# Expert weights from a PSUM bank, and the steps of dt by transfers, in a four-batch decoder kernel

## What is computed

```python
x = _layernorm(x + _L0_attn_ref(x, ...))            # state-space scan, 1024 channels x 16 states
x = _layernorm(x + _L0_xattn_ref(x, fside, ctx))    # two int8-quantised linears
x = _layernorm(x + _L0_ffn_ref(x, ...))             # gated feed-forward, 2048 hidden
x = _layernorm(x + _L1_attn_ref(x, ...))            # recurrence of another kind, 32 heads
x = _layernorm(x + _L1_xattn_ref(ctx, x, ...))      # state-space scan, 512 channels x 16 states
x = _layernorm(x + _L1_ffn_ref(x, ...))             # 8 experts of 352, top 2, and a shared one of 1408
```

```python
dt = softplus(ts @ dt_proj_w + dt_proj_b);  A = -exp(A_log)
h  = exp(dt_t * A) * h + (dt_t * x_t) * B_t          # for each position t
...
C   = top-2 routing weights of each token, one column for each of 8 experts
out = sum_e C[:, e] * swiglu_e(x) + sigmoid(x @ Wsg) * swiglu_shared(x)
```

## Time and profile before

| | |
|---|---|
| median of 3 runs | 4341.19 us (4337.18 to 4343.31) |
| profiled execution, its own time | 4338.52 us |
| its span | 4336.7 us |
| PE busy | 3493.1 us |
| DVE busy | 3340.8 us |
| ACT busy | 1365.5 us |
| POOL busy | 1277.1 us |
| granted clock, mean | 0.893 |

### The profile page before, as it was taken

How to read it: one execution, slowest core, us unless ns; L and a number is a source line. 1 busy time by engine, 2 the same in 40 slices (tenths; PEclk the granted TensorE clock), 3 DMA queues, 4 the chain that set the end, 5 groups by cost and what they waited for, 6 DMA issues and landing times. The chain is left out here.

```text
span 4336.7 us, 40016 instructions
## 1 busy us (share of the span) xinstructions
PE 3493.1 (81%) x14699; PEld 1469.8 (34%) x14967; DVE 3340.8 (77%) x2930; ACT 1365.5 (31%) x2006; POOL 1277.1 (29%) x452
## 2 busy tenths in 40 slices
PE   5777759887899859887899858877899968974898
PEld 2222233333333333333333333323333333322444
DVE  5998469777899668778899758868799858867444
ACT  4666333124322233224322233213422143121101
POOL 1544204331344203342244303343244312332000
PEclk9888879898899979989799978989799978976899
DMA  4888302121122302222122201122122301210232
GB/s 154 303 319 315 148 22 81 68 83 54 66 73 73 119 16 73 68 82 69 58 74 73 110 32 66 67 82 78 44 73 73 124 32 59 73 58 15 73 102 75
DMA packets 72917, 393.38 MB, mean 91 GB/s; under 512 B 8080, under 2 KB 8208, under 8 KB 70288
## 3 DMA queue, kind: packets, MB, share of 16 engines
q1 hardware_dynamic: 69264, 384.44, 25.5%
q10 hardware_dynamic: 3456, 6.29, 0.4%
HBM read 320.45 MB, written 70.25 MB: 90 GB/s over the span
## 5 line engine op out<-in xcount | busy, mean ns | idle before, releaser
L261 PE MATMUL ps<-r,ring 128*128 128x512 bf16 (+2 forms) x1989 | 781.4, 393 | 45.1 <-POOL r L244 22.5
L1025 POOL TENSOR_TENSOR hh<-hh,bc 128x2048 f32<-128x2048 f32 x72 | 337.2, 4683 | 1070.9 <-DVE hh L950 1070.9
L258 PE MATMUL ps<-r,ring 128*128 128x512 bf16 (+1 forms) x1349 | 540.4, 401 | 107.6 <-DVE xc L990 38.4
L258 PE MATMUL ps<-xr,ring 128*128 128x512 bf16 x1536 | 607.4, 395 | 11.5 <-DMA ring<-wsplit 8.8
L262 PE MATMUL ps<-xr,ring 128*128 128x512 bf16 x1533 | 604.2, 394 | 2.6
L262 PE MATMUL ps<-r,ring 128*128 128x512 bf16 (+2 forms) x1355 | 542.5, 401 | 2.0
L910 ACT ACTIVATE da<-ps,params_sb 128x511 f32<-128x511 f32 x768 | 463.2, 691 | 72.1 <-PE ps L816 33.6
L1025 POOL TENSOR_TENSOR bc<-bc 128x2048 f32<-128x2048 f32 x64 | 299.5, 4679 | 375.6 <-DVE bc L950 375.6
L1025 POOL TENSOR_TENSOR r<-r,bc 128x2048 f32<-128x2048 f32 x56 | 263.2, 4701 | 327.3 <-DVE r L950 327.3
L950 DVE TENSOR_TENSOR_SCAN hh<-da,hh 128x2048 f32<-128x2048 f32 x72 | 330.5, 4590 | 1.5
L917 ACT ACTIVATE row<-ps 128x512 f32<-128x512 f32 x100 | 59.7, 597 | 764.7 <-PE ps L262 764.7
(11 more groups left out here) (241 smaller groups left out, 6367.4 us busy)
## 6 DMA issues: line engine op xcount, KB each, us to landing
ring<-wsplit SPq DMA_DIRECT2D x304, 768.0 KB, 4.3
r<-wstream SPq DMA_DIRECT2D x76, 768.0 KB, 7.4
wsplit<-ring SPq DMA_DIRECT2D x58, 768.0 KB, 4.5
wsplit<-r SPq DMA_DIRECT2D x18, 768.0 KB, 5.7
r<-xT SPq DMA_DIRECT2D x7, 1024.0 KB, 4.8
r<-gates_dram SPq DMA_DIRECT2D x3, 2048.0 KB, 8.4
bc<-guwT SPq DMA_DIRECT2D x4, 1024.0 KB, 7.1
out<-xr SPq DMA_DIRECT2D x4, 1024.0 KB, 3.9
```

The costliest lines, as they stand in the source:

```text
L258: mm = pe.matmul(out, w_hi, x_hi, start=start, stop=False)
L261: pe.matmul(out, w_hi, x_lo, start=False, stop=False)
L1025: pool.tensor_tensor(quartet(s), quartet(s), k.out_rows, ALU.mult).then_inc(read, 1)
```

## The change

- `k.gates` (nine copies in SBUF) goes. `k.weight_rows` keeps the turned rows in SBUF, and in the expert stage PE spreads a tile's weights into a PSUM bank, from which `times_weight` reads. With scan steps this is bank 0 alone: `weight_spreads` lists the rows of the bank that change from one tile to the next (17 spreads over the 33 tiles), and `times_weight` is one instruction for each tile. A spread waits until the tile before has been multiplied. In the last batch three banks take turns, one spread for each of 9 experts, and `times_weight` keeps its pieces.
- Bank 0 was `dt_bank`. In the expert stage with scan steps dt now comes by transfers: ACT issues four of 32 rows for each step (`fetch`), into the first quarter of `da`, after scan(s-2); three exponentials read that quarter, and a fourth overwrites it once they are done. `a0` is rescaled by 1/16 once, before the batches, as the spread's factor is gone.
- In `hidden_and_scan`, `spread_dtx(1)` comes before `up(0)` rather than after it, in every stage.
- In `close_batch`: the nine spreads and nine copies go; dt products 4 and 5 with their `magnitude` and `positive` move ahead of the logits; the first half of the logits waits for half of the norm; the four low halves of the expert stage's input are made here, after line 1868, and no longer at the start of that stage; `logarithm(1)` comes before the copy of the rows.

```diff
+def weight_spreads(tile):
+    if tile == ROUTED:
+        return [(0, P, NEXP)]
+    if tile > ROUTED:
+        return []
+    held = lambda row: (tile * P - P + row) // FEXP if tile else None
+    return [(a, b, e) for a, b, e in expert_pieces(tile) if held(a) != e]
...
+            def spread_weights(jt):
+                q = 32 * ((jt + 3) % 4)
+                for a, b, e in new_weights(jt):
+                    if blocks and jt >= 1:
+                        pe.wait_ge(weighted, jt)
+                    elif not blocks and e >= 3:
+                        pe.wait_ge(weighted, expert_tiles(e - 3)[-1] + 1)
+                    pe.matmul(weight_bank(e)[a:b, :], k.ident[q:q + 32, q + e:q + e + 1].broadcast_to([32, b - a]),
+                              k.weight_rows[q:q + 32, :], start=True, stop=True).then_inc(spread_mm, 1)
...
+            if blocks and not carried:
+                spread_dt(1)
             if blocks:
-                spread_dt(1)
+                spread_dtx(1)
             if tiles:
                 up(0)
...
             for step in range(steps):
-                if step + 1 < blocks:
+                if 2 <= step + 1 < blocks:
                     spread_dtx(step + 1)
-                if step + 2 < blocks:
+                if step + 2 < blocks and not carried:
                     spread_dt(step + 2)
+                if gated and 1 <= step < tiles:
+                    spread_weights(step)
...
+            def fetch(s):
+                if s >= 2:
+                    act.wait_ge(scanned, s - 1)
+                rows = dt[32 * (s % 4):32 * (s % 4) + 32, s // 4, 1:T]
+                for g in range(4):
+                    act.dma_start(k.da[s % 2][32 * g:32 * g + 32, 0, 1:T], rows).then_inc(dt_in[s % 2], 16)
...
+                if carried:
+                    act.wait_ge(dt_in[s % 2], 64 * (s // 2 + 1))
+                    for n in range(1, GRP):
+                        a = exponential(n, k.da[s % 2][:, 0, 1:T])
+                    a.then_inc(others, 1)
+                    act.wait_ge(others, s + 1)
+                    exponential(0, k.da[s % 2][:, 0, 1:T]).then_inc(decay, 1)
+                    return
...
+            if carried:
+                fetch(0)
+                fetch(1)
...
                 if step + 1 < tiles:
                     gate_tanh(step + 1)
+                if carried and step + 2 < blocks:
+                    fetch(step + 2)
...
                 dve.wait_ge(hid, jt + 1)
+                dve.wait_ge(spread_mm, sum(len(new_weights(t)) for t in range(jt + 1)))
                 for a, b, e in weight_pieces(jt):
-                    op = dve.tensor_tensor(h[a:b, :], h[a:b, :], k.gates[a:b, e, :], ALU.mult)
+                    op = dve.tensor_tensor(h[a:b, :], h[a:b, :], weight_bank(e)[a:b, :], ALU.mult)
...
-            pe.wait_ge(after_states.out, 4)
+            if ahead:
+                s.dt_product(pe, 4)
+                s.dt_product(pe, 5)
             for c in range(4):
+                pe.wait_ge(after_states.out, 2 * (c // 2) + 2)
...
-            pe.wait_ge(rows_in, 1)
-            for e in range(NEXP + 1):
-                if e >= 4:
-                    pe.wait_ge(gcopy[e % 2], e // 2 - 1)
-                q = 32 * (e % 4)
-                pe.matmul(weight_bank(e), k.ident[q:q + 32, q + e:q + e + 1].broadcast_to([32, P]), weight_rows[q:q + 32, :],
-                          start=True, stop=True).then_inc(gmm, 1)
...
+                s.logarithm(act, 1)
             act.wait_ge(rows_mm, 1)
-            act.activation(weight_rows, k.ps[:, 1, :], ACT.Copy).then_inc(rows_in, 1)
-            for e in range(0, NEXP + 1, 2):
-                act.wait_ge(gmm, e + 1)
-                act.activation(k.gates[:, e, :], weight_bank(e), ACT.Copy).then_inc(gcopy[0], 1)
-            if ahead:
-                s.logarithm(act, 1)
+            act.activation(k.weight_rows, k.ps[:, 1, :], ACT.Copy)
...
             dve.memset(k.xc[:, 1, :], 0.0).then_inc(gates, 1)
+            for c in range(KM):
+                low(dve, k.moe_xlo[:, c, :], k.xr[:, c, :])
...
-            for e in range(1, NEXP + 1, 2):
-                dve.wait_ge(gmm, e + 1)
-                dve.tensor_copy(k.gates[:, e, :], weight_bank(e)).then_inc(gcopy[1], 1)
```

More of the change, by code:

```diff
@@ L763, in hidden_and_scan @@
         hidlo, xsplit, down, taken = [sem(n) for n in ("hidlo", "xsplit", "down", "taken")]
-        dt_mm, dtx_mm, decay = [sem(n) for n in ("dt_mm", "dtx_mm", "decay")]
+        dt_mm, dtx_mm, decay, others = [sem(n) for n in ("dt_mm", "dtx_mm", "decay", "others")]
+        dt_in = [sem(f"dt_in{i}") for i in range(2)]
+        spread_mm = sem("spread_mm")
         dtx_in, early_in = sem("dtx_in"), sem("early_in")
@@ L790, in quartet, with weight_bank, new_weights @@
             return states(s).rearrange("p (n t) -> p n t", n=GRP)
+        carried = gated and blocks > 0
+        def weight_bank(e):
+            return k.ps[:, 0 if blocks else e % 3, :]
+        def new_weights(jt):
+            if blocks:
+                return weight_spreads(jt)
+            return [(0, P, e) for e in range(NEXP + 1) if expert_tiles(e)[0] == jt]
         def weight_pieces(jt):
+            if blocks:
+                return [(0, P, 0)]
             return expert_pieces(jt) if jt < ROUTED else [(0, P, NEXP)]
@@ L798, in _ @@
                 k.w.load_until(sp, slot + blocks - 2, RING - 1, last)
-                sp.wait_ge(dt_mm, blocks)
+                for i in range(2):
+                    sp.wait_ge(dt_in[i], 64 * (blocks // 2))
                 sp.wait_ge(dtx_mm, blocks)
@@ L871, in down_piece @@
                     k.w.done()
+            def spread_weights(jt):
[8 more added lines that the diff above has]
+            if blocks and not carried:
+                spread_dt(0)
             if blocks:
-                spread_dt(0)
                 spread_dtx(0)
+            if gated:
+                spread_weights(0)
+            if tiles and not gated:
+                pe.wait_ge(xsplit, KM)
             if tiles:
-                pe.wait_ge(xsplit, KM)
                 gate(0)
+            if blocks and not carried:
+                spread_dt(1)
             if blocks:
-                spread_dt(1)
+                spread_dtx(1)
             if tiles:
@@ L904, in _, with exponential @@
         def _(act):
-            def decays(s):
+            def fetch(s):
[4 more added lines that the diff above has]
+                    act.dma_start(k.da[s % 2][32 * g:32 * g + 32, 0, 1:T], rows).then_inc(dt_in[s % 2], 16)
+            def decays(s):
+                def exponential(n, source):
+                    return act.activation(k.da[s % 2][:, n, 1:T], source, ACT.Exp, scale=rate[:, GRP * s + n:GRP * s + n + 1])
+                if carried:
[6 more added lines that the diff above has]
+                    return
                 act.wait_ge(dt_mm, s + 1)
@@ L909, in decays @@
                 for n in range(GRP):
-                    a = act.activation(k.da[s % 2][:, n, 1:T], dt_bank[:, 1:T], ACT.Exp, scale=rate[:, GRP * s + n:GRP * s + n + 1])
+                    a = exponential(n, dt_bank[:, 1:T])
                 a.then_inc(decay, 1)
@@ L993, in _ @@
                 inputs_of(0)
-            if tiles:
+            if tiles and not gated:
                 for c in range(KM):
@@ L1623, in close_batch @@
         mixed, turned, zg, yz = [sem(n) for n in ("mixed", "turned", "zg", "yz")]
-        logits, st, ex, exd, sgd, gates, rows_mm, rows_in, gmm, *gcopy = [
-            sem(n) for n in ("logits", "st", "ex", "exd", "sgd", "gates", "rows_mm", "rows_in", "gmm", "gcopy_act", "gcopy_dve")]
+        logits, st, ex, exd, sgd, gates, rows_mm = [
+            sem(n) for n in ("logits", "st", "ex", "exd", "sgd", "gates", "rows_mm")]
         stats = ([k.ps[:, 4 + h, 0:HT] for h in range(2)], [k.ps[:, h, 0:HT] for h in range(2)])
@@ L1704, in _ @@
             if ahead:
-                for j in range(4, J0):
-                    s.dt_product(pe, j)
+                s.dt_product(pe, 6)
+                s.dt_product(pe, 7)
             pe.wait_ge(gates, 2)
```

19 lines of the change are left out of this document (10 added, 9 removed).

## The result

| | median, us | runs |
|---|---|---|
| before | 4339.18 | 4336.85 to 4343.31, 4 runs |
| after | 4293.23 | 4290.6 to 4296.68, 4 runs |
| ratio | 0.9894 | 95% interval 0.9876 to 0.9911 |

The change is worth 46 us, not 85, and 4293 lies above the range of 4235 to 4288. The sign was right; nearly half of the gain is missing. The profiled execution has a span of 4288.8 us, against 4336.7.

What follows compares the result with a forecast made beforehand. DVE was taken to bound the expert stage of batches 1 to 3, PE the last. Sum: 3 x (15.3 - 1.5 + 9.3 + 2.6) + 4 x 1.9 + 0.3 = 85.0 us, from 4341.2 to 4256, range 4235 to 4288.

Steps and rivals of the forecast that it cites:

- a): Expert stage, batches 1 to 3: the multiply by the weight no longer waits for POOL; gain 15.3 us a batch.
- b): Expert stage, batches 1 to 3: PE just keeps up with faster DVE; loss 1.5 us a batch, between 0 and 7.
- c): Closing stage, batches 1 to 3: totals end 8.3 us earlier, logits' followers about 1 more; gain 9.3 a batch.
- d): Start of expert stage, batches 1 to 3: wait for dtx(1) goes, transfers delay scan(0); net gain 2.6 us, 0 to 4.5.
- e): Later steps of the expert stage: dt transfers stay hidden, cost 0, unless a landing takes over 5.1 us.
- f): Feed-forward stage, all four batches: DVE's 3.39 us wait for dtx(1) goes; gain 1.9 us each, between 0 and 2.7.
- g): Last batch: closing stage 8.3 us and logits 1.2 earlier, PE's added spreads cost 9.2; net gain 0.3 us.
- rival 1: PE becomes the bound of the expert stage: half of the multiply's gain goes, 4280 us; chance 0.17.
- rival 3: Slower: transfers become ACT's pace if landings average over 5.1 us; 4438 us at 7 us; chance 0.03.
- Rival 2: Line 976 stays long since its SBUF operand isn't the cause: multiply gains only 5.5 us, 4285 us; chance 0.05.

Runs made afterwards that it cites:

- experiment 2: Kernel after without the weight spreads of tiles 1 to 32 in batches 1 to 3 (other experts' weights left out): 4263.83 us, ratio to before 0.9817.
- experiment 9: Kernel after with one full-width spread for each cut tile, right weights kept through constant matrices: 4274.25 us, ratio to before 0.9844.
- Experiment 8: Kernel after with late ring slots ahead of early loads, step 1's transfers behind step 0's exponentials, weights' spread between gate and up: 4283.34 us, ratio to before 0.9862.
- experiment 1: Kernel after with the two late slots of the weight ring issued ahead of the next stage's early loads: 4272.68 us, ratio to before 0.9843.
- the best version: Kernel after with late ring slots ahead of early loads, step 1's transfers behind step 0's exponentials, full-width spreads with right weights: 4247.17 us, ratio to before 0.9772.
- Experiment 4: Kernel before with dt products 4 and 5 ahead of the logits, half of the norm's wait, low halves moved; nine copies kept: 4322.94 us, ratio 0.9962.
- Experiment 5: Kernel after with the transfers for step 1 issued behind the exponentials of step 0: 4278.66 us, ratio to before 0.985.
- Experiment 3: Kernel before with only the spread of dtx for step 1 put ahead of the first up product, in all stages: 4333.54 us, ratio 0.9984.
- experiment 12: Kernel before with only the two late slots of the weight ring issued ahead of the next stage's early loads: 4333.32 us, ratio 0.9979.

## Why the prediction was wrong

By the terms of its sum, us for all batches. The measured ones are those of the table of stretches, and of experiments 2 and 9 where a) and b) are told apart. Four things failed: b), d), f), and the end of the expert stage, which the sum doesn't have. c) came close.

| term | forecast | measured |
|---|---|---|
| a) multiply by the weight | 3 x 15.3 | 3 x 15.2 |
| b) PE follows | -3 x 1.5 | -3 x 6.5 |
| c) closing stage | 3 x 9.3 | 3 x 8.4 |
| d) start of the expert stage | 3 x 2.6 | 3 x 0.3 |
| e) transfers in the steps | 0 | 0 |
| f) feed-forward stage, with the mixer behind it | 4 x 1.9 | 4 x 0.1 |
| g) last batch | 0.3 | 1.5 |
| end of the expert stage | not in the sum | -3 x 3.9 |
| sum | 85.0 | 42.4 |

**a) held,** and so did its cause. The Trainium skill's rule on two SBUF operands ("SBUF — State Buffer", SBUF: two separate sides) agrees: with one operand in PSUM the multiply took 0.69 us beside a working POOL. POOL's hold did not move to the low part (0.69 us at 1136.16).

**b) failed,** in this step: the weights' spread "takes its place and costs as little, except where tile 8 and tile 19 need two". It was read off a pair of spreads of 128 columns, which ran at one time. Eight of the 17 spreads have 32 or 64 columns, and those ran behind dtx's spread, for 1.0 us each (one of 64 columns from 1146.88 to 1147.88, with dtx's begun at 1145.83): 8 a batch, of which 6.5 were felt. Experiments 2 and 9 settle it: without spreads and with full-width ones the middle is the same 309.3. Why a narrow one can't run beside dtx's, no run shows. So rival 1 came true, with its size (6.5 felt, 7 foreseen) by luck and not by its reason: PE's lateness after `reduce_quad` cost nothing that shows, since 309.3 is as short as a) alone makes it. Experiment 8 is the same cause from the other side: a spread without a neighbour costs PE its whole length, whatever its width.

**The end of the stage was missed.** The chain of the last slots of the ring was not looked at, because PE's idle time there, 2.80 us, was small. When the steps got faster, SP issued its early loads as before, but PE came to the slot behind them 6.6 us after its issue rather than 7.0, and the slot landed after 11.6 us rather than 9.7, behind a load of `gates_dram` that took 10.6 rather than 8.4. The wait grew by 2.3 us, and PE came out of it at its lower clock; experiment 1 takes all of it away. Why the load of `gates_dram` itself took longer is not known: with full-width spreads it took 8.7 and with no spreads 8.5, in the best version 10.7.

**c) came close, but not as worked out.** The part that the nine copies gave, line 1895 to the last `total`, is 7.7 us, where 8.3 was forecast. Of the 1.0 for the logits 0.7 came (16.9 to 16.2), and 2.2 in the last batch. But the logits did not start 1.3 us later. They started at 1066.24, 4.68 us after DVE began the norm's last step (1061.56); before, that was 2.54. The two dt products ahead of them and the logits themselves (6.83 us) ran at the lower clock; the gain is that less stood behind them, 4.7 us to line 1962 and not 7.9 to line 1895. The low halves were hidden, as said: DVE still waits 2.27 us for the logits.

```profile
1061.56 2.48 DVE L1176 TENSOR_TENSOR xr<-xc,row 128x512 f32<-128x512 f32 x4
...
1068.40 2.42 DVE L259 TENSOR_TENSOR r<-xr 128x512 bf16<-128x512 f32 x4
...
1073.10 0.19 DVE L1940 TENSOR_REDUCE xc<-ps 128x4 f32<-128x32 f32 x1 [2.27 <-PE ps L1776]
...
1066.24 6.83 PE L1776 MATMUL ps<-params_sb,xr 128*128 128x9 f32 x32
```

Experiment 4 shows what this order gives when PE has its upper clock there: logits of 3.63 us that start 2.53 after the norm's last step, and 13.7 us to line 1902, its line 1895. Of the 27 such stages in the kernel after and in the eight experiments built on it that keep this order, six were like that. In them the stretch to line 1962 was 13.7 and the one to the last `total` 6.9, not 16.2 and 8.3: 3.9 us a batch, with no edit there. So a shift of up to 3.9 us a batch comes and goes by the clock, and it is in the sums of experiments 1, 2, 5, 8 and 9. What decides which clock PE has there is not shown.

**f) failed,** in the step that took the gain inside the stage (2.2, where 1.9 was forecast) for a net gain and put what stands behind the stage at nothing. Of the 2.2 us 0.4 is lost up to the next norm and 1.7 from there to the closing norm. Experiment 3, which has this edit and none in the mixer or the closing stage, loses the same. So do all 44 stages of the eleven kernels that have the edit (2.0 to 2.2). Of the twelve stages without it (the kernel before, experiments 4 and 12) nine lose nothing; the other three lose 0.8 to 3.4 us. The first 0.8 us of the loss in the mixer can be seen. PE starts there after a long wait, at the lower clock, and gets the upper one later than before. Before, timeline of PE:

```profile
841.77 0.63 PE L261 MATMUL ps<-bc,ring 128*128 128x512 bf16 x1 [9.31 <-POOL bc L244]
...
844.98 0.41 PE L262 MATMUL ps<-bc,ring 128*128 128x512 bf16 x1
```

after:

```profile
834.02 0.59 PE L273 MATMUL ps<-bc,ring 128*128 128x512 bf16 x1 [8.93 <-POOL bc L259]
...
839.57 0.40 PE L273 MATMUL ps<-bc,ring 128*128 128x512 bf16 x1
```

and in experiment 3:

```profile
840.91 0.58 PE L258 MATMUL ps<-bc,ring 128*128 128x512 bf16 x1 [8.93 <-POOL bc L244]
...
846.44 0.40 PE L258 MATMUL ps<-bc,ring 128*128 128x512 bf16 x1
```

Eight matmuls of 0.42 us before (the record of the first is missing; its weight load stands at 841.36), twelve in the other two: four at 0.2 us more are the 0.8. That the clock is the cause of the whole loss is argued from such rows, not shown.

**d) was mis-sized,** by one duration: an issue of a 32-row transfer between parts of SBUF took 0.60 to 0.62 us on ACT, not the 0.35 of a 256 KB store to DRAM. The forecast's 2.8 us were 5.1. Experiment 5 takes four of the eight off the path and gets 2.5 back.

**e) held.** A transfer of 64 KB landed 2.0 us after its issue (median), and the four of a step 3.8 us after the first one's issue; in the middle of the stage DVE waited for no exponential; rival 3 did not come. The Trainium skill's port figure ("SBUF — State Buffer", Door 1: the DMA port swizzle) had led to an estimate of 3.4 us for the 256 KB of a step together; the 3.8 measured for the four is near it, and holds 1.9 us in which the other three were issued. An issue of 0.61 was four times charged to ACT in each step too, 1.0 us more than forecast, and hidden.

**g)** was a little better than forecast: the last batch gained 2.2 us from the norm to line 1895 (1.2 forecast) and 6.3 before the fifth piece of down, and gave 6.9 back in PE's expert stage.

Rival 2 is out. The range failed at its bad end: that took b) at 7, d) at 0 and f) at 0, close to what came, but kept c) whole (2.7 us too much) and had nothing for the end of the stage, 11.7 us.

## What to carry to other kernels

An operation that runs for nothing beside another does so only in the shape in which it was seen: read the rows of that shape, or give the new one the same shape, as the constant matrices of experiment 9 do. When a stage gets faster, follow its last transfers too: a slot that is issued behind the next stage's loads is late by more than the time won. Follow a gain past the end of its stage: f)'s was measured in full there and gone by the next closing norm. And take the price of a transfer's issue from one of the same kind and count all that stand ahead of the first work of a stage.

## What the runs showed that was not expected

- Of two float32 matmuls in different 32 rows of the array, both ran at one time when both had 128 columns; one of 32 or 64 columns began only when the other was done (1178.81 behind 1177.76).
- An issue of 64 KB between parts of SBUF cost ACT 0.60 to 0.62 us at the start of the stage, and 0.35 for 256 KB to DRAM.
- A 768 KB load behind 2.5 MB on the same queue landed in 11.6 us (9.7 before the change) instead of 4.2, and the 5.07 us that PE stood for it cost the upper clock as well.
- The same 32 matmuls of the router's logits took 3.63 us in some stages and 6.83 in others of the same code, at a granted clock of 1.00 and 0.50; with what hangs on them that is 3.9 us a batch.
